# Writing the q and k stacks to memory as a finished image: more and narrower writes, fewer and wider reads

## The reference, cut to what matters

```python
k, q, v = proj(W_key), proj(W_query), proj(W_value)      # (b, 16 heads, 512, 16)
scores = jnp.einsum('bhqd,bhkd->bhqk', q, k) * hd ** (-0.5)
scores = jnp.where(causal, scores, -jnp.inf)
out = jnp.einsum('bhqk,bhkd->bhqd', jax.nn.softmax(scores, axis=-1), v)
...
x = _layernorm(x + attention(x))
scores_t = jnp.swapaxes(jax.nn.softmax(x @ router_w.T), 1, 2)
gate_vals, sel_idx = jax.lax.top_k(scores_t, capacity)   # 129 tokens for each expert
out = out.at[b_idx, sel_idx].add(expert(x[b_idx, sel_idx]) * gate_vals)
x = _layernorm(x + out)
```

## Time and profile before

| what | value |
| --- | --- |
| median of 3 runs | 968.99 us (968.87 to 969.45) |
| the profiled execution | 969.03 us, span 967.3 us |
| TensorE busy in matmuls | 836.3 us (86%) |
| VectorE, ScalarE, GpSimd busy | 660.6, 520.5, 523.2 us |
| SP's own DMA queue (q1) | 72560 packets, 77.92 MB |
| writes `part_d<-w_raw` | 96 of 128 KB |
| reads `w_parts<-part_d` | 192 of 128 KB |

### The profile page before, as it was taken

How to read it: one execution, slowest core, us unless ns; L and a number is a source line. 1 busy time by engine, 2 the same in 40 slices (tenths; PEclk the granted TensorE clock), 3 DMA queues, 4 the chain that set the end, 5 groups by cost and what they waited for, 6 DMA issues and landing times. The chain is left out here.

```text
span 967.3 us, 17022 instructions
## 1 busy us (share of the span) xinstructions
PE 836.3 (86%) x5864; PEld 627.4 (65%) x5864; DVE 660.6 (68%) x2017; ACT 520.5 (54%) x1010; POOL 523.2 (54%) x622
## 2 busy tenths in 40 slices
PE   4769999999999999977666999998989899898990
PEld 3444454545455454433365989998989899898990
DVE  4467788787878788999759945555474735546464
ACT  2137666666675757544354445564545556454555
POOL 5347565656565653323655256757375645637344
PEclk9769999999999999988878899999999999998996
DMA  4996767687787778201052224325242332422248
GB/s 140 171 172 122 126 125 149 119 144 140 143 144 144 121 143 177 67 2 45 24 200 81 45 42 89 91 40 131 35 125 45 92 64 51 120 34 33 39 125 257
DMA packets 90102, 100.52 MB, mean 104 GB/s; under 512 B 8736, under 2 KB 83488, under 8 KB 89888
## 3 DMA queue, kind: packets, MB, share of 16 engines
q1 hardware_dynamic: 72560, 77.92, 37.6%
q0 software_dynamic: 12800, 16.92, 10.5%
q10 hardware_dynamic: 4656, 4.59, 1.5%
HBM read 65.38 MB, written 33.62 MB: 102 GB/s over the span
## 5 line engine op out<-in xcount | busy, mean ns | idle before, releaser
L510 DVE CUSTOM_DVE_ANT_0 n_ps<-n_ps,tri 128x512 f32<-128x512 f32 (+3 forms) x512 | 238.5, 517 | 75.3 <-PE n_ps L642 73.8
L1080 DVE TENSOR_TENSOR h_lo<-g,h_hi 128x384 fp32r<-128x384 f32 (+1 forms) x184 | 155.2, 851 | 126.3 <-ACT h_hi L1016 126.0
L430 ACT ACTIVATE pt<-st_ps 128x512 f32<-128x512 f32 x320 | 183.9, 601 | 76.0 <-PE st_ps L627 60.9
L1156 PE MATMUL y_ps<-w_parts,h_hi 128*128 128x256 f32 (+1 forms) x1152 | 213.3, 280 | 0.0
L1011 ACT ACTIVATE g<-h_ps,b 128x384 f32<-128x384 f32 (+1 forms) x192 | 104.2, 543 | 197.8 <-PE h_ps L1142 194.9
L1142 PE MATMUL h_ps<-tt_hi,w_parts 128*128 128x384 f32 (+1 forms) x768 | 179.1, 338 | 32.1 <-issue 21.5
L375 POOL TENSOR_SCALAR_AFFINE_SELECT pt<-pt 128x256 f32<-128x256 f32 (+1 forms) x320 | 111.6, 365 | 130.8 <-ACT pt L430 129.8
L1156 PEld LDWEIGHTS y_ps<-w_parts,h_hi 128*128 128x128 f32 (+1 forms) x1152 | 172.4, 178 | 3.3 <-ACT h_hi L1016 0.2
L983 POOL DMA_INDIRECT acc<-y,tok_no x64 | 102.3, 1599 | 120.6 <-DVE y L1094 112.4
L1156 PE MATMUL y_ps<-w_parts,h_lo 128*128 128x256 f32 (+1 forms) x576 | 161.0, 280 | 0.0
L1142 PEld LDWEIGHTS h_ps<-tt_hi,w_parts 128*128 128x128 f32 x768 | 133.6, 200 | 34.4 <-issue 33.2
(11 more groups left out here) (157 smaller groups left out, 1106.1 us busy)
## 6 DMA issues: line engine op xcount, KB each, us to landing
w_parts<-part_d SPq DMA_DIRECT2D x192, 128.0 KB, 6.1
w_raw<-in_w SPq DMA_DIRECT2D x16, 1024.0 KB, 5.6
part_d<-w_raw SPq DMA_DIRECT2D x96, 128.0 KB, 6.1
w_raw<-in_xt SPq DMA_DIRECT2D x8, 512.0 KB, 5.0
res<-in_x SPq DMA_DIRECT2D x8, 512.0 KB, 10.1
x<-res SPq DMA_DIRECT2D x8, 512.0 KB, 7.0
acc<-res SPq DMA_DIRECT2D x8, 512.0 KB, 8.2
fin<-acc SPq DMA_DIRECT2D x4, 512.0 KB, 3.9
```

The lines of the kernel that those rows point to most:

```text
L430: nc.scalar.activation(pt[:, slot % PT_RING, n % UP, :], st_ps[at % ST_RING][:, :], ACT.Exp, scale=S_SCALE).then_inc(exp_done, 1)
L510: ins = nc.vector.tensor_tensor_reduce(out=src[:, h, :], in0=src[:, h, :], in1=mask, scale=-1.0, scalar=-BIG_NEG, op0=ALU.add, op1=ALU.min ...
L1080: nc.vector.tensor_tensor(h_lo[:, q % 2, n, 0:cols], g[:, at % G_RING, 0:cols], h_hi[:, q % 2, n, 0:cols].bitcast(F32), ALU.subtract).then ...
L1156: ins = nc.tensor.matmul(y_ps[at % Y_RING][0:rows, 0:C], x[:, q % 2, m, toks], w[e % 2][:, m, :], start=i == 0, stop=i == len(terms) - 1)
```

## The change

Memory no longer holds the parts but the stacks themselves. `image_d` has for q and k, for both batch slots and both halves, 96 rows by 8 heads by 512 tokens. Each part is written once for every block that holds it: six transfers for a tile instead of three, each 128 KB, to 16 rows of the image for each of the 8 heads. A stack is then read with one transfer of 96 rows by four heads (a quarter, 4 KB a row): four transfers of 384 KB for a half instead of twelve of 128 KB. The semaphore `stack_in` is kept for each quarter, so TensorE's `nat` units wait at each quarter, and the counts of `parts_out` are 96 where they were 48.

```diff
-    part_d = nc.dram_tensor("part_d", [2, 2, 3, 2, P, T], BF16).ap()
+    image_d = nc.dram_tensor("image_d", [2, 2, 2, KQ, HH, T], BF16).ap()
...
                 for part in range(3):
-                    sp.dma_start(part_d[which, b % 2, part, half_, :, :], parts[:, tile % 2, part, :]).then_inc(parts_out[tile % 2], 16)
+                    for at, held in enumerate((Q_PARTS, K_PARTS)[which]):
+                        if held == part:
+                            to = image_d[which, b % 2, half_, at * D:(at + 1) * D, :, :].rearrange("d h n -> h d n")
+                            sp.dma_start(to, parts[:, tile % 2, part, :]).then_inc(parts_out[tile % 2], 16)
             elif stage == "stack":
 
                 for parity in range(2):
-                    sp.wait_ge(parts_out[parity], 48 * (2 * b + n + 1))
+                    sp.wait_ge(parts_out[parity], 16 * WRITES * (2 * b + n + 1))
...
-                for which, stack, blocks in ((0, qst, Q_PARTS), (1, kst, K_PARTS)):
-                    for at, part in enumerate(blocks):
-                        src = part_d[which, b % 2, part, n, :, :].rearrange("(h d) n -> d h n", d=D)
-                        sp.dma_start(stack[at * D:(at + 1) * D, b % 2, HH * n:HH * (n + 1), :], src).then_inc(stack_in[n][b % 2], 16)
+                for quarter in (2 * n, 2 * n + 1):
+                    heads = slice(4 * (quarter % 2), 4 * (quarter % 2) + 4)
+                    for which, stack in ((0, qst), (1, kst)):
+                        sp.dma_start(stack[0:KQ, b % 2, 4 * quarter:4 * quarter + 4, :],
+                                     image_d[which, b % 2, n, :, heads, :]).then_inc(stack_in[quarter][b % 2], 16)
...
-                if n % (NU // 2) == 0:
-                    pe.wait_ge(stack_in[n // (NU // 2)][b % 2], 16 * BLOCKS * (b // 2 + 1))
+                if n % N_QUARTER == 0:
+                    pe.wait_ge(stack_in[n // N_QUARTER][b % 2], 32 * (b // 2 + 1))
```

More of the change, by code:

```diff
@@ L34 @@
 Q_PARTS = (0, 1, 0, 1, 2, 0)
-BLOCKS = len(K_PARTS) + len(Q_PARTS)
+WRITES = len(K_PARTS)
 KQ = len(K_PARTS) * D
@@ L244, in attention @@
     parts_out = [sem("parts_out0"), sem("parts_out1")]
-    stack_in = [[sem(f"stack{h}{p}") for p in range(2)] for h in range(2)]
+    stack_in = [[sem(f"stack{q}{p}") for p in range(2)] for q in range(4)]
     nat_done = sem("nat_done")
@@ L313, in _ @@
                 if b >= 2:
-                    sp.wait_ge(stack_in[half_][b % 2], 16 * BLOCKS * (b // 2))
+                    for quarter in (2 * half_, 2 * half_ + 1):
+                        sp.wait_ge(stack_in[quarter][b % 2], 32 * (b // 2))
                 for part in range(3):
-                    sp.dma_start(part_d[which, b % 2, part, half_, :, :], parts[:, tile % 2, part, :]).then_inc(parts_out[tile % 2], 16)
+                    for at, held in enumerate((Q_PARTS, K_PARTS)[which]):
+                        if held == part:
+                            to = image_d[which, b % 2, half_, at * D:(at + 1) * D, :, :].rearrange("d h n -> h d n")
+                            sp.dma_start(to, parts[:, tile % 2, part, :]).then_inc(parts_out[tile % 2], 16)
             elif stage == "stack":
                 for parity in range(2):
-                    sp.wait_ge(parts_out[parity], 48 * (2 * b + n + 1))
+                    sp.wait_ge(parts_out[parity], 16 * WRITES * (2 * b + n + 1))
                 if b >= 2:
                     sp.wait_ge(st_done, ((b - 2) * PAIRS + 4 * (n + 1)) * UP)
-                for which, stack, blocks in ((0, qst, Q_PARTS), (1, kst, K_PARTS)):
-                    for at, part in enumerate(blocks):
-                        src = part_d[which, b % 2, part, n, :, :].rearrange("(h d) n -> d h n", d=D)
-                        sp.dma_start(stack[at * D:(at + 1) * D, b % 2, HH * n:HH * (n + 1), :], src).then_inc(stack_in[n][b % 2], 16)
+                for quarter in (2 * n, 2 * n + 1):
[3 more added lines that the diff above has]
+                                     image_d[which, b % 2, n, :, heads, :]).then_inc(stack_in[quarter][b % 2], 16)
                 if (b, n) == (B - 1, 1):
@@ L382, in _ @@
                 pool.wait_ge(qk_rest, tile)
-                pool.wait_ge(parts_out[tile % 2], 48 * (tile // 2))
+                pool.wait_ge(parts_out[tile % 2], 16 * WRITES * (tile // 2))
                 link(nc.gpsimd.tensor_tensor(qk_r[:, :], qk_f[:, tile % 2, :], parts[:, tile % 2, 0, :], ALU.subtract))
@@ L453, in _ @@
                     act.wait_ge(qk_rest, tile - 1)
-                    act.wait_ge(parts_out[tile % 2], 48 * (tile // 2))
+                    act.wait_ge(parts_out[tile % 2], 16 * WRITES * (tile // 2))
                 nc.scalar.activation(parts[:, tile % 2, 0, :], ps[:, :], ACT.Copy).then_inc(qk_first, 1)
@@ L519, in _ @@
                 if n >= 2:
-                    dve.wait_ge(parts_out[n % 2], 48 * (n // 2))
+                    dve.wait_ge(parts_out[n % 2], 16 * WRITES * (n // 2))
                 link(nc.vector.tensor_tensor(qk_r[:, :], qk_f[:, n % 2, :], parts[:, n % 2, 0, :], ALU.subtract))
```

## The result

The changed kernel takes 977.29 us (median of 5 executions, 972.5 to 978.86), 8.3 us more than before: ratio 1.0085, 95% interval 1.0062 to 1.0108. Measured again beside the experiments it gave 1.0099 (1.0066 to 1.0132). The forecast was 980.2 us in a range of 968.5 to 993.

What follows compares the result with a forecast made beforehand. The prediction took a chain of SP's transfers to bound the start and engines to pace each iteration after it. 969.03 us plus 11.2 in the start, nothing in steady iterations, gave 980.2 us, range 968.5 to 993.

Steps and rivals of the forecast that it cites:

- Where the loss lies: Start, before the first `st` matmul: a chain of transfers, second v of batch 1 11.2 us later; steady iterations lose nothing.
- Eight engines for a write: Image writes in SP's queue: each runs on 8 engines, not 16, giving 64368 packets for q1.
- The price of a write on eight engines, 0.96 us: Each 128 KB image write in the start's chain: 0.96 us, between bounds of 0.735 and 1.47 us.
- free writes: Rival for the start: image writes do not crowd and take 0.735 us; second v +3.2 us, total 972.2 us; chance 0.25.
- the slow reads: Old 128 KB reads into 16 partitions: 136 GB/s, 0.96 us each; the same pace was assumed for the new writes.
- The price of a wide read, 1.1 us: Each 384 KB read to 96 partitions: 1.1 us at 360 GB/s, so 4.4 us a half, where it cost 11.5.
- The faster rival: Rival for the start: all 16 engines write, 0.37 us a write, issue paces at 0.47; total 965.2 us; chance 0.08.

Runs made afterwards that it cites:

- e9_dmajor_eight: Kernel of e1_dmajor with a free row after each 16 in the image, so writes run on eight engines again: 976.92 us, ratio 1.0097.
- e1_dmajor: Changed kernel with a tile's channels ordered (channel, head), so each write is one contiguous piece on 16 engines: 962.97 us, ratio 0.9935 to the kernel before.
- e8_half_rows_32_96: Kernel of e1_dmajor with a half read in four transfers, rows 32 to 95 and 0 to 31, all eight heads: 963.8 us, ratio 0.9963.
- e1_again: Second measurement of e1_dmajor, unaltered, beside other experiments: 963.89 us, ratio 0.996 to the kernel before.

## Why the prediction was right

The direction and the mechanism were right: a chain of transfers in the start, made longer by writes on eight engines. Two prices in the sum were wrong, and the total came near since they pull opposite ways. That part is luck.

**Where the loss lies.** Right. The start is a chain of transfers, and iterations have room. The steady load was put at 37.7 of 50.33 us for the eight engines; no transfer wait appeared in an iteration.

**Eight engines for a write.** Right, by the packets that were counted ahead (64368) and by `e9_dmajor_eight`. The packet count of ScalarE's queue was enough for it, and the rule of the Trainium skill (DMA: Bandwidth & Descriptors, "Why a DMA increments its semaphore by 16 and not by 1") agrees.

**The price of a write on eight engines, 0.96 us.** This term was mis-sized: 0.69 once running, the "free writes" case. The analogy to the slow reads failed. Only tile 0's six writes took near 1.0 us each (issue at 16.71, copy at 23.67, about 1.0 us of it latency); tile 1's took 4.08/6 = 0.68. Over the 36 writes of the chain that is some 8 us too much. By the rule of the Trainium skill (SBUF — State Buffer, "Door 1: The DMA port swizzle") eight engines that walk through their partitions in step would stand on four ports at a time, an estimated 109 GB/s; the writes here moved 189, so the trace does not bear out that they stay in step. One way to understand it, not tested: engines that visit the same ports one after another stop meeting once they are out of step.

**The price of a wide read, 1.1 us.** Mis-sized the other way: 6.7 us a half instead of 4.4, 4.6 us more over two halves. I took the pace of a load to 128 partitions for one to 96.

**How the errors met.** Tile 6 was copied at 58.06, where 58.5 was said: by then too dear writes and too cheap reads cancel. Tile 7 was copied at 62.15 instead of 64.3. The two errors and smaller delays between them leave 9.1 us for the first `st` where 11.2 was said, and 8.3 in the median. The free-writes rival, with the same cheap reads, would have said 972.2, 5.1 us under the 977.29 measured, against 2.9 over it for the forecast. It had the price of a write nearly right and still came out further off.

**The faster rival.** Its arithmetic was right, its condition was not met: `e1_dmajor` met it and gave 963 to 964 where 965.2 was said.

## What to carry to other kernels

In these runs a transfer's outermost count decided how many DMA engines carried it: a write with 8 outermost ran on eight, one with 128 on all 16. Count the closing packets of a queue to learn it, and choose the order of channels so that a write has all its 128 rows outermost. Destinations of 16 partitions moved about 130 GB/s with rows of 1 KB and of 8 KB, so here wide reads were worth doubled writes, but only when the writes kept all engines. Where a pipeline begins, price the chain of transfers with measured rates and replay the kernel before with them first. When a stage moves in one profile, look at the granted clock before giving it to the change.

## What the hardware showed that I had not expected

- Eight engines that each walk through 16 neighbouring partitions moved 151 GB/s in the first 4 us of writes and 189 GB/s later, with writes of the same form.
- A 96-partition read moved 231 GB/s (changed kernel, rows of 4 KB). By the time of a 4 KB packet, two splits of it differ: 0.217 us with rows 32 to 95 and 0 to 31, 0.265 us with rows 0 to 63 and 64 to 95.
- The same 20 matmuls of the v stage in the start took 2.70 us at a granted clock of 1.00 (`e8_half_rows_32_96`) and 4.92 us at 0.50 (`e1_again`), which moved the first `st` by more than the change in the reads did. The medians of the two kernels are the same.
